# A recurrent layer with routed experts: the plan's wide counts on VectorE, and Pool adding y before it fetches x

## What is computed

```python
xn = layernorm(x)                                  # x: 8 x 1024 x 256, float32
A  = sigmoid(log_A)
h_t = A * h_(t-1) + (xn @ B_w.T + B_b)             # 256 states
s  = h @ C_w.T + C_b
w, e = top_k(xn @ Wr + br, 2); w = softmax(w)      # 8 experts, 2 for each token
y  = sum over the two of w * (silu(xn @ W1[e]) * (xn @ W3[e])) @ W2[e]
out = x + s * silu(y)
```

## Time and profile before

| | |
|---|---|
| median of 3 runs | 815.08 us (814.54 to 815.41) |
| the profiled execution: its own time | 813.25 us |
| its span, first to last instruction | 811.3 us |
| TensorE busy | 771.4 us (95%), 5399 matmuls |
| VectorE busy | 516.8 us (64%) |
| Pool busy | 480.4 us (59%), 498 instructions |
| ScalarE busy | 375.7 us (46%) |
| mean granted clock of TensorE | 0.991 |
| chain that ended last | TensorE 80%, VectorE 8%, Pool 5%, issue 3%, DMA 2% |

### The profile page before, as it was taken

The page is one execution under the profiler, slowest core; times in us unless marked ns, Lnnn a source line. Parts: engine busy times, 40 slices in busy tenths (PEclk is TensorE's granted clock), DMA queues, the critical chain, the costliest instruction groups (busy, mean ns, idle before and its releaser), DMA issues.

```text
span 811.3 us, 17142 instructions
## 1 busy us (share of the span) xinstructions
PE 771.4 (95%) x5399; PEld 689.9 (85%) x5399; DVE 516.8 (64%) x1084; ACT 375.7 (46%) x665; POOL 480.4 (59%) x498
## 2 busy tenths in 40 slices
PE   2999889599999999999999999999999999999997
PEld 1554448599999999999999999999999999998786
DVE  6878964276767766765786565446555765553576
ACT  3984244154555544544554454435444644443440
POOL 4741838778658656865787378467646866554000
PEclk9999999889999999999999999999999999999999
DMA  9979813154464545433654454354346554952995
GB/s 293 345 257 321 149 30 102 54 110 73 105 164 67 131 61 130 72 63 53 186 91 79 111 133 78 53 125 77 65 115 159 118 117 80 320 112 33 273 368 201
DMA packets 101842, 111.02 MB, mean 137 GB/s; under 512 B 15634, under 2 KB 89236, under 8 KB 101748
## 3 DMA queue, kind: packets, MB, share of 16 engines
q0 software_dynamic: 25920, 35.54, 26.3%
q1 hardware_dynamic: 50032, 50.34, 19.4%
q10 hardware_dynamic: 25796, 24.20, 10.0%
HBM read 66.61 MB, written 43.45 MB: 136 GB/s over the span
## 4 chain that ended last, share of the span: by engine, by line
PE 80%; DVE 8%; POOL 5%; issue 3%; DMA 2%; ACT 1%; ACTq 1%; DVEq 0%; POOLq 0%; SPq 0%
PE bank L1484 14%; PE bank L1458 14%; PE bank L1457 14%; PE bank L1456 14%; PE bank L1485 7%; PE bank L1588 5%; PE bank L1445 3%; PE bank L1358 3%; DVE xnT L1060 2%; PE bank L1322 2%; POOL xg L583 1%; DVE stats L926 1%; PE bank L1334 1%; PE bank L1510 1%; DVE xnT L1072 1%
## 5 line engine op out<-in xcount | busy, mean ns | idle before, releaser
L592 POOL DMA_INDIRECT y_rows<-y_sb,token_at x128 | 217.8, 1702 | 143.6 <-DVE y_sb L1176 84.1
L1456 PE MATMUL bank<-xh,W_sb 128*128 128x256 f32 x1024 | 288.1, 281 | 3.5 <-DVE xl L1126 3.0
L1457 PE MATMUL bank<-xh,W_sb 128*128 128x256 f32 x1024 | 286.6, 280 | 0.0
L1458 PE MATMUL bank<-xl,W_sb 128*128 128x256 f32 x1024 | 286.6, 280 | 0.0
L1484 PE MATMUL bank<-W_sb,hh 128*128 128x512 f32 x512 | 191.1, 411 | 9.2 <-DVE y_sb L1176 9.2
L1456 PEld LDWEIGHTS bank<-xh,W_sb 128*128 128x128 f32 x1024 | 192.9, 188 | 6.0 <-issue 3.9
L1457 PEld LDWEIGHTS bank<-xh,W_sb 128*128 128x128 f32 x1024 | 193.1, 189 | 0.0
L1458 PEld LDWEIGHTS bank<-xl,W_sb 128*128 128x128 f32 x1024 | 192.5, 188 | 0.0
L1164 DVE TENSOR_TENSOR hbuf<-hbuf,bank 128x512 f32<-128x512 f32 x128 | 87.3, 687 | 153.0 <-PE bank L1458 132.0
L583 POOL DMA_INDIRECT xg<-xn_rows,token_at x128 | 144.4, 1128 | 37.2 <-issue 18.9
L1485 PE MATMUL bank<-W_sb,hl 128*128 128x256 f32 x512 | 144.8, 283 | 0.0
(11 more groups left out here) (249 smaller groups left out, 924.5 us busy)
## 6 DMA issues: line engine op xcount, KB each, us to landing
x_late<-L_attn_x SPq DMA_DIRECT2D x24, 512.0 KB, 8.8
raw<-L_ffn_W ACTq DMA_DIRECT2D x24, 512.0 KB
odd_raw<-L_ffn_W ACTq DMA_DIRECT2D x21, 512.0 KB
xn_rows<-h_sb SPq DMA_DIRECT2D x16, 512.0 KB, 5.7
y_rows<-xnT SPq DMA_DIRECT2D x4, 2048.0 KB, 15.1
yy<-y_rows SPq DMA_DIRECT2D x16, 512.0 KB, 9.3
out<-x_late SPq DMA_DIRECT2D x11, 512.0 KB, 7.3
x_kept<-L_attn_x SPq DMA_DIRECT2D x4, 512.0 KB, 6.9
```

The costliest lines, as they stand in the source:

```text
L592: return eng.indirect_dma_start(out=y_rows, out_offset=rows, in_=y, in_offset=None, bounds_check=T + TW - 1, oob_is_err=True, compute_op=A ...
L1456: eng.matmul(part, high, x_h, start=k == 0, stop=False)
L1457: eng.matmul(part, low, x_h, start=False, stop=False)
L1458: last = eng.matmul(part, high, x_l, start=False, stop=k == KD - 1)
```

## The change

On Pool, the two wide counts of `rest_of_plan` and the count of owners are gone, as is the running sum of odd_of. VectorE makes all four, with a comparison and a reduction for each count and one scan, behind the low parts of the first weights and ahead of its first switch; Pool waits for them (counts_ready). They have working places of their own. The odd part of the plan is cut in two: first the experts of the odd half tiles, with one count of odd_plan_ready, then their columns, with the second. ScalarE's odd_load waits for the first only; VectorE waits for the second before the odd piece of tile 4. In Pool's loop, all tiles but the first now have their scatter first and the gather of the tile four on behind it. The diff, cut to its core (the places and semaphores that are only declared are left out):

```diff
-        plan_f, plan_no, compared = plan_place(PLAN), plan_place(EXT + 1), plan_place(EXT * E)
+        plan_f, plan_no, compared, matched = plan_place(PLAN), plan_place(EXT + 1), plan_place((E + 1) * E), plan_place(2 * E * E)
+        odds_compared, switches_compared = plan_place((EXT - XG_RING) * E), plan_place((PAIR_TILES - XG_RING) * E)
+        owner_compared = plan_place(4 * E)
...
             def rest_of_plan():
 
-                count(odds_until[:, first:EXT], plan_no[:, first + 1:EXT + 1], odd_from)
+                eng.wait_ge(counts_ready, 4)
                 columns_of(first, PAIR_TILES)
-                count(switches[:, first + 1:PAIR_TILES + 1], plan_no[:, first + 1:PAIR_TILES + 1], first_at)
                 switches_of(first, PAIR_TILES)
...
-            def odd_plan():
-
-                link(eng.memset(odds_before[:, 0:1], 0.0))
-                for e in range(1, E):
-                    link(eng.tensor_tensor(odds_before[:, e:e + 1], odds_before[:, e - 1:e], odd_of[:, e - 1:e], ALU.add))
...
+            place, unused = plan_no[:, 0:E], SLOT_TILES - 1.0
+            same, weighed = (matched[:, n * E * E:(n + 1) * E * E].rearrange("p (j e) -> p j e", e=E) for n in range(2))
+            columns = plan_f[:, COLUMN_AT + PAIR_TILES:COLUMN_AT + PAIR_TILES + E]
+            experts = plan_f[:, ODD_EXPERT_AT:ODD_EXPERT_AT + E]
+
+            def add_matched(out, of):
+
+                link(eng.tensor_tensor(weighed, same, of.unsqueeze(1).broadcast_to([P, E, E]), ALU.mult))
+                link(eng.tensor_tensor(weighed[:, :, 0:4], weighed[:, :, 0:4], weighed[:, :, 4:8], ALU.add))
+                link(eng.tensor_tensor(weighed[:, :, 0:2], weighed[:, :, 0:2], weighed[:, :, 2:4], ALU.add))
+                for n in range(2):
+                    link(eng.tensor_tensor(out, out, weighed[:, :, n], ALU.add))
+
+            def odd_experts():
+
+                link(eng.tensor_tensor(odds_before, odd_ends, odd_of, ALU.subtract))
                 link(eng.tensor_scalar(overflow, pair_ends[:, E - 1:E], 2.0, -2.0 * PAIR_TILES, ALU.mult, ALU.add))
                 link(eng.tensor_tensor(overflow, overflow, odd_of[:, E - 1:E], ALU.add))
                 link(eng.tensor_scalar(overflow, overflow, 0.0, None, ALU.max))
-                place, unused = plan_no[:, 0:E], SLOT_TILES - 1.0
                 link(eng.tensor_scalar(place_of, odds_before, overflow, None, ALU.add))
+                link(eng.tensor_scalar(over, place, overflow, None, ALU.is_lt))
+                link(eng.tensor_tensor(expert_of, odd_of, place, ALU.mult))
+                link(eng.memset(expert_of[:, E - 1:E], 0.0))
+                link(eng.tensor_tensor(in_twos(experts), in_twos(over), two_each(owner), ALU.mult))
+                link(eng.tensor_tensor(same, place.unsqueeze(2).broadcast_to([P, E, E]), place_of.unsqueeze(1).broadcast_to([P, E, E]), ALU.subtract))
+                link(eng.tensor_tensor(same, same, same, ALU.mult))
+                link(eng.tensor_scalar(same, same, -1.0, 1.0, ALU.mult, ALU.add))
+                link(eng.tensor_scalar(same, same, 0.0, None, ALU.max))
+                add_matched(experts, expert_of)
+                eng.tensor_copy(plan[:, ODD_EXPERT_AT:ODD_EXPERT_AT + E], experts).then_inc(odd_plan_ready, 1)
+
+            def odd_columns():
+
                 link(eng.tensor_scalar(column_of, pair_ends, 2.0, -unused, ALU.mult, ALU.add))
                 link(eng.tensor_tensor(column_of, column_of, odds_before, ALU.add))
                 link(eng.tensor_tensor(column_of, column_of, odd_of, ALU.mult))
                 link(eng.memset(column_of[:, E - 1:E], 0.0))
-                link(eng.tensor_tensor(expert_of, odd_of, place, ALU.mult))
-                link(eng.memset(expert_of[:, E - 1:E], 0.0))
-                link(eng.tensor_scalar(over, place, overflow, None, ALU.is_lt))
-                link(eng.tensor_copy(odd_from, pair_ends))
-                link(eng.memset(odd_from[:, E - 1:E], 1000.0))
-                count(owner, plan_no[:, PAIR_TILES + 1:EXT + 1], odd_from)
-
-                def two_each(v):
-                    return v.unsqueeze(2).broadcast_to([P, 4, 2])
-
-                def in_twos(v):
-                    return v.rearrange("p (a b) -> p a b", b=2)
-
-                columns = plan_f[:, COLUMN_AT + PAIR_TILES:COLUMN_AT + PAIR_TILES + E]
-                experts = plan_f[:, ODD_EXPERT_AT:ODD_EXPERT_AT + E]
                 link(eng.tensor_tensor(in_twos(columns), in_twos(place), two_each(odds_until[:, PAIR_TILES:EXT]), ALU.add))
                 link(eng.tensor_scalar(columns, columns, 2.0 * PAIR_TILES - unused, None, ALU.add))
                 link(eng.tensor_tensor(columns, columns, over, ALU.mult))
                 link(eng.tensor_scalar(columns, columns, unused, None, ALU.add))
-                link(eng.tensor_tensor(in_twos(experts), in_twos(over), two_each(owner), ALU.mult))
-                each = compared[:, 0:2 * E * E].rearrange("p (s j e) -> p s j e", s=2, e=E)
-                same, weighed = each[:, 0, :, :], each[:, 1, :, :]
-                link(eng.tensor_tensor(same, place.unsqueeze(2).broadcast_to([P, E, E]), place_of.unsqueeze(1).broadcast_to([P, E, E]), ALU.subtract))
-                link(eng.tensor_tensor(same, same, same, ALU.mult))
-                link(eng.tensor_scalar(same, same, -1.0, 1.0, ALU.mult, ALU.add))
-                link(eng.tensor_scalar(same, same, 0.0, None, ALU.max))
-                for out, of in ((columns, column_of), (experts, expert_of)):
-                    link(eng.tensor_tensor(weighed, same, of.unsqueeze(1).broadcast_to([P, E, E]), ALU.mult))
-                    link(eng.tensor_tensor(weighed[:, :, 0:4], weighed[:, :, 0:4], weighed[:, :, 4:8], ALU.add))
-                    link(eng.tensor_tensor(weighed[:, :, 0:2], weighed[:, :, 0:2], weighed[:, :, 2:4], ALU.add))
-                    for n in range(2):
-                        link(eng.tensor_tensor(out, out, weighed[:, :, n], ALU.add))
-                for a, b in ((COLUMN_AT + PAIR_TILES, COLUMN_AT + PAIR_TILES + E), (ODD_EXPERT_AT, ODD_EXPERT_AT + E)):
-                    eng.tensor_copy(plan[:, a:b], plan_f[:, a:b]).then_inc(odd_plan_ready, 1)
+                add_matched(columns, column_of)
+                eng.tensor_copy(plan[:, COLUMN_AT + PAIR_TILES:COLUMN_AT + PAIR_TILES + E], columns).then_inc(odd_plan_ready, 1)
...
             for i in range(PAIR_TILES):
                 n, j = i % GROUP, i // GROUP
-                if i + XG_RING < PAIR_TILES:
+                if i == 0:
                     wait_apart(eng, slot_weighed, i + 1)
                     gather(i + XG_RING)
-                if i == 0:
-                    odd_plan()
+                    odd_experts()
+                    odd_columns()
                     eng.wait_ge(odd_plan_ready, 2)
                     odd_gather(0)
                 if n == 5 and j + 1 < ODD_TILES:
                     wait_apart(eng, odd_weighed, j + 1)
                     odd_gather(j + 1)
                 scatter(i)
+                if i and i + XG_RING < PAIR_TILES:
+                    wait_apart(eng, slot_weighed, i + 1)
+                    gather(i + XG_RING)
                 if n == GROUP - 1 and j < ODD_TILES:
                     odd_scatter(j)
...
-                wait_apart(eng, odd_plan_ready, 2)
+                wait_apart(eng, odd_plan_ready, 1)
...
+                    if isinstance(j, int):
+                        eng.wait_ge(odd_plan_ready, 2)
...
+            def count(out, numbers, limits, scratch):
+
+                n, of = numbers.shape[1], limits.shape[1]
+                each = scratch[:, 0:n * of].rearrange("p (n e) -> p n e", e=of)
+                link(eng.tensor_tensor(each, numbers.unsqueeze(2).broadcast_to([P, n, of]), limits.unsqueeze(1).broadcast_to([P, n, of]), ALU.is_ge))
+                eng.tensor_reduce(out, each, AX.X, ALU.add).then_inc(counts_ready, 1)
+
+            few = XG_RING
+            count(odds_until[:, few:EXT], plan_no[:, few:EXT], odd_from, odds_compared)
+            count(switches[:, few + 1:PAIR_TILES + 1], plan_no[:, few:PAIR_TILES], first_at, switches_compared)
+            count(owner, plan_no[:, PAIR_TILES:EXT], pair_ends[:, 0:E - 1], owner_compared)
+            eng.tensor_tensor_scan(odd_ends, plan_no[:, 1:2].broadcast_to([P, E]), odd_of, 0.0, ALU.mult, ALU.add).then_inc(counts_ready, 1)
```

8 lines of the change are left out of this document (6 added, 2 removed).

## The result

The changed kernel takes **839.33 us** (median of 4 runs, 833.81 to 841.42), the kernel before in the same series 815.25 (814.54 to 816.68): a ratio of 1.0283 [1.0231, 1.0334], slower by 24 us. The prediction was 825.6 with a range to 834: the right side, and more than half of the loss missing (10.5 us forecast on top of the kernel before, 24.1 measured). The profiled execution is the fastest of the four, 833.81 us with a span of 832.0 (before 811.3), so its trace has to account for 20.7 us; 5.5 more lie between it and the median.

What follows compares the result with a forecast made beforehand. It took TensorE, busy 771.4 of 811.3 us, to bound the kernel. -11.3 + 0.6 + 14.7 + 4.5 + 2 = +10.5 us on the profiled 813.25 gave 823.8, plus 1.8 to the median 825.6 us; range 808 to 834.

Steps and rivals of the forecast that it cites:

- The stop, -11.3 us: TensorE's stop before the down product, from Pool's late odd plan holding ScalarE, goes whole: -11.3 us.
- Rival (d): Plan still late for ScalarE's odd_load because VectorE's counts come late: 828 to 836 us, chance 0.04.
- VectorE's counts, +0.6: VectorE's compares delay Pool's second gather of tile 0: +0.6 us, bounds 0 and 0.9; by the port rule +1.5.
- The late rows, 14.7: Gathers behind scatters bring x late to TensorE, mostly at group starts (tiles 12, 21, 36, 52): 14.7 us.
- slow landings, +4.5: Rows land slower beside the next expert's weight loads, 0.9 us more at five places: +4.5 us.
- Where Pool waits for y that is harmless: Gathers one Pool turn later cost nothing where Pool waits for y; 3 to 6 us margin in a group's second half.
- These stalls add up: TensorE's stalls for late rows sum, since each moves TensorE and with it y and Pool alike.
- the row's 2.80 us: Tile 0's second gather, issue to TensorE's use: measured 2.80 us kept over an estimated 2.3, which would give about 820.
- The clock, +2: One or two longer TensorE stalls each bring a clock fall to 0.50: +2 us, bounds 0 and 7.
- From the profile to the median, +1.8: Median of the runs lies 1.8 us above the profiled execution, added to 823.8 for 825.6 us.
- Rival (c): Cascade: slow landings at each group's start, 3 us each, and a clock fall with each: 841 us, chance 0.08.
- Rivals (a) and (b): Late rows cost less than the stop, 813 us, chance 0.16; the order costs nothing, 804 us, chance 0.07.

Runs made afterwards that it cites:

- e6: Plan's part of the change alone, old order in Pool's loop, with VectorE's counts moved behind its low parts of tile 0's x and W2: 805.24 us.
- e1: Changed kernel with the old order of Pool's loop (gather, then scatter) in every tile, the plan's part kept: 805.43 us, ratio 0.9883.
- the second execution: Changed kernel profiled once more, unchanged: one execution of 836.21 us, span 834.5.
- e10: Changed kernel without the odd half tiles' weight loads after the first, so its output is not the reference's there: 833.89 us, ratio 1.0236.
- e5: Changed kernel with the new order only at tiles n = 2 to 7 of each group, gather first at n = 0 and 1: 819.9 us, ratio 1.0061.
- e4: Changed kernel with eight unused products on TensorE ahead of the transposes of tiles 12, 20, 28, 36, 44 and 52: 840.93 us, ratio 1.0322.
- e8: Plan's part alone, old order in Pool's loop, with unused products where TensorE stands around tile 0: 803.71 us, ratio 0.9847.
- e1_again: Plan's part of the change alone, old order in Pool's loop, in a second series: 804.35 us, ratio 0.986.

## Where the prediction was right and where it failed

The plan's half came as forecast. What failed is the price of the new order: 21.2 us forecast (14.7 for late rows, 4.5 for slow landings, 2 for the clock), 33.5 to 35.6 measured. The points below say which steps of it, and what is still open.

- **The stop, -11.3 us: right.** The plan alone gives -9.4, -11.4 and (e6) -9.2. The times along Pool held within 1 us: gather of tile 4 begun at 128.8 in e1 (forecast 128.4), the experts written by 138.5 (139.5), the columns by 144.1 (144). odd_load runs at 148.10 with 2.79 us before y_low, where the earlier trace rows had 15.02. Rival (d) is out.
- **VectorE's counts, +0.6: mis-sized, harmless.** 0.35 us on the gather. In the changed kernel two of the three compares ran beside that gather (0.65 us from 115.67 and 0.17 from 116.93, the gather from 115.85 to 117.18). The port lock that the Trainium skill describes ("SBUF — State Buffer", on the shared port pair) shows in its direction (0.98 to 1.33 and back in e6), not in a price of 1.5 us.
- **The late rows, 14.7, and slow landings, +4.5: the sum fits the profiled execution by luck, the parts don't.** New waits are 19.5 us there (21.5 less tile 0's 2.0), forecast 19.2; but that execution is the fastest of its four, and the second one has 24.2. Place by place, tiles 5, 12, 20 with 21, and 52 came as forecast (1.61, 2.64, 2.39, 2.85 against 1.1, 2.5, 2.8 and 3.0 with tile 53). Tile 36 came with 0.53 against 3.1, tile 28 with 2.03 against some 0.5; tiles 30 and 35, for which none was forecast, have 1.92 and 2.09, tiles 44 and 60, "in time by 1 to 2 us", 1.23 and 1.90. If each of the twelve waits is cut by what its landing took over the quiet 1.87 us (tile 60: 5.36 - 1.87, more than its whole wait), 9.4 us are left, and 10.1 belong to landings (11.6 and 12.6 in the second execution). So **the slow landings were mis-sized**, 4.5 against 10.1: the delay was taken from tile 0, with 0.9 more at five places, and the loads cost up to 3.5 each, at more places. That cut is arithmetic along a trace; e10 shows that landings recover, but neither the waits nor the time do.
- **"Where Pool waits for y that is harmless", with 3 to 6 us of margin in the second half of a group: this step failed.** With the new order only at n = 2 to 7 of each group, where the prediction had one late tile of some 0.5 us (tile 62), e5 loses 14.9 us against the plan alone. Five of its six new waits are at tiles gathered behind n = 2 (6, 14, 22, 30 and 54), the sixth is tile 35, in the second half. Tile 35 shows best what was passed over. Its gather stands behind the scatter of tile 31, and this one ended, before the change, at 457.80:

```profile
456.22 1.58 POOL L592 DMA_INDIRECT y_rows<-y_sb,token_at  x1 [0.30 <-issue]
```

By the prediction's own arithmetic 457.80 + 4.64 = 462.44, against TensorE's transposes at 462.25 in the trace before: no margin at all. Every run with the new order there has a wait of 1.8 to 2.5 us at this tile.

- **"These stalls add up": they don't.** The two halves of the order cost 28.2 and 14.9 us alone and 33.5 together, and stalls filled at the groups' starts (e4) came back at other tiles. So a list of places, each priced against the old times, can come near the sum of one execution, but it does not say what removing one of them is worth.
- **Keeping the row's 2.80 us from issue to use, and not less, was right.** It was 2.85 us in e10's tile 44 (555.43 to 558.28) and 6.34 in the changed kernel's tile 60 (712.10 to 718.44). The estimate of 2.3 us by the fit in the Trainium skill, "DMA: Bandwidth & Descriptors", on the anatomy of one DMA, has terms for the DMA itself alone; the time of 820 that came with it would have been farther off.
- **The clock, +2: mis-sized.** TensorE's busy time is 7.2 us over the plan-only kernel's 772.9 in the first profile and 5.3 in the second. "One or two" falls were counted; four came in mid-span in the first and three in the second. 7 was this term's upper bound.
- **From the profile to the median, +1.8: mis-sized.** That was carried over from the kernel before. The late rows have their own spread, 4.7 us of waits between two executions, and the median lies 5.5 above the first. All in all the order costs 33.5 to 35.6 us where its terms had 21.2. New waits and added busy time together are 26.7 us in the first execution (833.81) and 29.5 in the second (836.21); what the last 3 us up to the median are made of no trace shows.
- **Rival (c), 841, had the time**, and 0.08 was too little. Its clock term of 7 came (5.3 and 7.2). Its 15 us of slow landings at the groups' starts did not: by the cut above they are 7.0 us in the first execution (5.1 at tiles 12, 20, 28, 36, 44 and 52 together, 1.9 at tile 60), and with the loads there left out (e10) the kernel still loses 19.8 us. So its number came nearer than its mechanism.
- Rivals (a) and (b) are out: new waits of 19.5 us, over their turning point of 11.

## What to carry to other kernels

An instruction that waits for a landing delays all that is queued behind it on its engine, so a prefetch belongs ahead of it, even where that engine is only 59% busy. Price a fetch's landing beside the loads that really run in that slot, since the quiet value was a third of the worst one; and look for margins at every tile, not only where the queue is known to stand. Where a change lives on margins of 1 to 3 us at many places, expect the places to change with each execution, and take the spread of the median from that, not from the kernel before.

## What the runs showed of the hardware

- A gather's rows were used 1.9 us after it ended with a DMA share of 0.27 (tile 37), and 4.2 and 5.4 us with 0.86 and 1.10 (tiles 44 and 60). With the odd half tiles' loads left out (e10) tiles 28, 44 and 52 were at 1.9, and had been at 3.8, 4.2 and 2.8.
- Stretches at the lower clock behind a wait for rows lasted 3.4 or 6.8 us where the wait had been 1.9 to 3.2 us; but not each such wait brought one (1.92 at 417.04 did not). Holding the clock by fillers brought TensorE forward at the head (from tile 0's transposes to tile 3's 24.6 us in e8 and 27.1 in e1_again, 1.2 net of the later start) and gained nothing where the rows were late anyway (e4).
- Tile 0's second gather beside VectorE's compares and reductions took 1.33 us (1.32 and 1.33 in two more executions), and 0.98 without them (e6).
